# Attention of one item beside the feed-forward of the item two behind, in one order for all engines, with SiLU through tanh

## Time and profile before

| | us |
|---|---|
| median of 3 runs | 1201.09 |
| lowest, highest | 1197.25, 1201.25 |
| the profiled execution | 1206.52 |
| its span | 1204.7 |
| mean granted clock of TensorE | 0.762 |

### The profile page before, as it was taken

The page is one execution under the profiler, slowest core; times in us unless marked ns, Lnnn a source line. Parts: engine busy times, 40 slices in busy tenths (PEclk is TensorE's granted clock), DMA queues, the critical chain, the costliest instruction groups (busy, mean ns, idle before and its releaser), DMA issues. The chain is left out here.

```text
span 1204.7 us, 14263 instructions
## 1 busy us (share of the span) xinstructions
PE 1005.4 (83%) x5034; PEld 656.7 (55%) x5034; DVE 552.0 (46%) x1203; ACT 440.4 (37%) x649; POOL 261.5 (22%) x375
## 2 busy tenths in 40 slices
PE   3788777858658888779999788788789999999986
PEld 3534333225534444338888563433348888888874
DVE  2644453313344454424554544454434454534458
ACT  2344443332205434452343225444442332322240
POOL 7201032214314442211110104241110010101044
PEclk9666675567766555568999995655579999999997
DMA  5001010110001101110000002201210000000001
GB/s 126 2 1 19 1 19 2 18 18 16 1 0 54 37 1 36 36 18 9 1 1 1 1 13 64 43 14 35 40 21 5 1 1 1 1 1 1 1 1 35
DMA packets 24715, 21.01 MB, mean 17 GB/s; under 512 B 6559, under 2 KB 19847, under 8 KB 24519
## 3 DMA queue, kind: packets, MB, share of 16 engines
q1 hardware_dynamic: 24647, 20.10, 7.8%
...
HBM read 12.33 MB, written 1.05 MB: 11 GB/s over the span
## 5 line engine op out<-in xcount | busy, mean ns | idle before, releaser
L1134 DVE TENSOR_REDUCE mneg<-PS 128x4 f32<-128x624 f32 (+1 forms) x192 | 170.7, 894 | 180.5 <-PE PS L751 180.2
L1546 ACT ACTIVATE work<-PS 104x1024 f32<-104x1024 f32 (+1 forms) x160 | 163.5, 1022 | 182.4 <-PE PS L833 180.6
L1286 DVE TENSOR_TENSOR work<-PS,work 128x512 f32<-128x512 f32 (+2 forms) x168 | 114.8, 685 | 211.4 <-PE PS L885 134.9
L1576 ACT ACTIVATE work<-PS 128x512 f32<-128x512 f32 (+2 forms) x168 | 99.9, 597 | 243.5 <-PE PS L885 241.5
L902 PEld LDWEIGHTS PS<-down_w,work 128*128 128x128 f32 (+2 forms) x1472 | 175.4, 194 | 6.2 <-DVE work L1286 1.0
L902 PE MATMUL PS<-down_w,work 128*128 128x128 f32 (+2 forms) x1472 | 175.9, 277 | 0.7 <-DVE work L1286 0.7
L883 PE MATMUL PS<-xh_sb,arena 128*128 128x512 f32 (+2 forms) x352 | 152.6, 433 | 9.5 <-DVE work L1286 9.2
L848 PE MATMUL PS<-work,vb_sb 104*32 104x512 f32 (+1 forms) x640 | 147.6, 1014 | 3.4 <-ACT work L1546 3.4
L885 PE MATMUL PS<-xh_sb,arena 128*128 128x512 f32 (+2 forms) x352 | 142.8, 406 | 0.0
L884 PE MATMUL PS<-xl_sb,arena 128*128 128x512 f32 (+2 forms) x352 | 142.4, 405 | 0.0
L751 PE MATMUL PS<-kb_sb,qxt_sb 49*128 49x312 f32 x256 | 69.5, 530 | 57.9 <-DVE mneg L1134 52.7
...
## 6 DMA issues: line engine op xcount, KB each, us to landing
...
```

The source lines that it names most:

```text
L1134: dve.tensor_reduce(to, PS[:, bank:bank + 2, 0:HB * head_width(layer)].rearrange("p f (n h) -> p f h n", h=HB), AX.X, ALU.max, negate=True ...
L1286: dve.tensor_tensor(HH[0:rows, e % 2, j, :], PS[0:rows, 2 * (n % 2) + 1, :], SS[0:rows, n % 2, :], ALU.mult).then_inc(*sig["h"].mark((i, n)))
L1546: act.activation(P[0:rows, m % P_RING, :, :], PS[0:rows, 0:2, :], ACT.Exp, scale=SCALE).then_inc(*sig["p"].mark((i, m)))
L1576: act.activation(SS[0:rows, n % 2, :], PS[0:rows, bank, :], ACT.Silu).then_inc(*sig["act"].mark((i, n)))
```

## The change

`plan`, `all_slots` and the loops over `ITEMS` go. `step_pieces(s)` lists the pieces of one of 15 steps with a place for each, sorted by place, and each engine runs this one list. Step s holds attention item s (for s up to 11) and feed-forward item s - 2 (for s from 2 to 13), with the layer norm and preparation of attention item s + 1, parts of s + 2, and the end of attention s - 1 with the preparation of its feed-forward. The items of layer 3 are placed in steps 12, 13 and 14.

Banks: scores 0 and 1 as before; maxima, transposes, projections and router 2 and 3; values 4 alone (the score pairs are reordered so that one half of the heads is finished and evacuated before the other); first product of a tile 5 alone, second 6, both for GELU in turn; down projection 7 alone. `hidden` and the tanh output get space of their own, and `xn` and `xT` have one place for attentions and one for feed-forwards. The splits of the weights move to steps 4 to 10 (`w`), with the down weights of layer 2 in six groups (`wd`), each behind the last reader of the place that it takes; SP's queue issues them in the order of the list. SiLU is computed as 0.5 x (1 + tanh(0.5 x)): Tanh on ScalarE, then `silu` and the product on VectorE. The start of the kernel (the preparation of items 0 and 1) stays but for its banks. The space that the program keeps for DMA descriptors made at run time is set to 1024 bytes.

```diff
+N_ATT = 3 * B
+SKEW = 2
+N_STEPS = N_ATT + SKEW + 1
+BANK_MX, BANK_PV, BANK_UP, BANK_Y, BANK_F3 = 2, 4, 5, 7, 0
...
+def attention_pieces(a, put):
+    i = item_of(a)
+    N, C = n_slots(i), quads(i)
+    W = width(a)
+    scale = W / 29.0
+    for m in range(N // 2):
+        put(2 * m, "st", i, m)
+    for u in range(2 * C):
+        put(4 * u + 5, "pv", i, u)
+    put(4 * C + 2.5, "evac", i, 0)
+    put(N + 3, "evac", i, 1)
+    if a + 1 < N_ATT:
+        n, j = a + 1, item_of(a + 1)
+        if a == 0:
+            put(0.1, "kt", n)
+        for h in range(HB):
+            put(h + 0.2, "kb", n, h)
+        if n < B:
+            first, last = 5.1, N - 0.9
+            for g in range(G):
+                put(1.2 + g, "qxt", n, g)
+        else:
+            if n >= 2 * B:
+                for t in range(T):
+                    put(1.4, "ln", j, t)
+                put(1.5, "norm", j)
+            at = (4.2, 5.2, 5.3, 6.2, 6.3, 8.1, 8.3, 8.4) if n >= 2 * B else (1.4, 2.4, 2.5, 3.4, 3.5, 5.4, 5.8, 5.9)
+            for x, name in zip(at, ("xt", "q", "q1", "q2", "q3", "q4", "qsplit", "qlow")):
+                put(x, name, j if name == "xt" else n)
+            qx = 9.6 if n >= 2 * B else 8.4
+            for g in range(G):
+                put(qx + 0.7 * g, "qxt", n, g)
+            first, last = qx + 3.0, N + 2.4
+        for m in range(N_MAX):
+            put(first + m * (last - first) / N_MAX, "max", n, m)
+        put(first + (N_MAX - MT_LAST + 0.6) * (last - first) / N_MAX, "mt", n, 0)
+        put(N + 2.7, "mt", n, 1)
+        put(N + 1.5, "v", n)
+    if a + 2 < N_ATT:
+        n, j = a + 2, item_of(a + 2)
+        for x, name in ((10.3, "kproj"), (10.4, "k1"), (12.4, "k2"), (13.4, "k3"), (N - 2.2, "ksplit"), (N - 1.2, "klow"), (N + 4, "kt")):
+            put(x, name, n)
+        if n < B:
+            for t in range(T):
+                put(0.3 + t, "ln", j, t)
+            put(3.3, "norm", j)
+            for x, name in ((7.2, "xt"), (9.1, "q"), (9.2, "q1"), (11.1, "q2"), (12.1, "q3"), (16.1, "q4"), (17.1, "qsplit"), (18.1, "qlow")):
+                put(x, name, j if name == "xt" else n)
+        elif n < 2 * B:
+            for t in range(T):
+                put(20.5 * scale, "ln", j, t)
+            put(20.6 * scale, "norm", j)
+def ffn_pieces(f, W, put):
+    i = ffn_item(f)
+    kind = ITEMS[i][0]
+    tiles = ffn_tiles(kind)
+    if kind == "F0":
+        for n in range(4):
+            put(1.7 + 2.2 * n, "up", i, n, 0)
+        put(W * 0.45, "down", i, 0)
+        put(W * 0.45 + 1, "acc", i, 0)
+        return
+    for n in range(len(tiles)):
+        put(W * (n + 0.3) / len(tiles), "up", i, n, 0)
+        put(W * (n + 0.55) / len(tiles), "silu", i, n)
+        put(W * (n + 0.8) / len(tiles), "up", i, n, 1)
+    for e in range(tiles[-1][0] + 1):
+        last = max(n for n, tl in enumerate(tiles) if tl[0] == e)
+        x = W * (last + 2.1) / len(tiles)
+        put(x, "down", i, e)
+        put(x + 0.3, "acc", i, e)
+def ffn_prepared(f, W, put):
+    j = ffn_item(f)
+    s = W / 29.0
+    for t in range(T):
+        put(11.5 * s, "ln", j, t)
+    put(11.6 * s, "norm", j)
+    if ITEMS[j][0] == "F0":
+        put(14.2 * s, "rows", j)
+    put(15.2 * s, "xt", j)
+    put(15.3 * s, "after_xt", j)
+    for n, x in enumerate((18.3, 20.0, 22.0)):
+        put(x * s, "late", j, n)
+def step_pieces(s):
+    placed = []
+    def put(x, *piece):
+        placed.append((x, len(placed), piece))
+    W = width(s)
+    if s in (2, 6):
+        put(1.3, "bv", s // 4 + 1)
...
+    if s < N_ATT:
+        attention_pieces(s, put)
+    if SKEW <= s < N_ATT + SKEW:
+        ffn_pieces(s - SKEW, W, put)
+    if 1 <= s <= N_ATT:
+        j = item_of(s - 1)
         for t in range(T):
+            put(3.1 + t, "recip", j, t)
+        put(7.3, "normal", j)
+        put(9.3, "finish", j)
+        ffn_prepared(s - 1, W, put)
+    if s == 12:
+        attention3_pieces(0, 0.8, put)
+        ffn3_pieces(0, 23.6, 30.0, put)
+    if s == 13:
+        attention3_pieces(1, 0.8, put)
+        attention3_pieces(2, 9.0, put)
+        ffn3_pieces(1, 9.9, 17.0, put)
+        ffn3_pieces(2, 18.0, 25.0, put)
+    if s == 14:
+        attention3_pieces(3, 0.8, put)
+        ffn3_pieces(3, 9.0, 16.0, put)
+    return [piece for _, _, piece in sorted(placed, key=lambda p: p[:2])]
...
+            def up(i, kt, m):
                 kind, layer, b = ITEMS[i]
-                e, col, rows, slot = ffn_tiles(kind)[kt]
-                bank = 2 * (kt % 2)
-                if kt == 0:
+                tiles = ffn_tiles(kind)
+                e, col, rows, slot = tiles[kt]
+                j = kt - min(n for n, tl in enumerate(tiles) if tl[0] == e)
+                bank = BANK_UP + (kt % 2 if kind == "F0" else 0)
+                if kt == 0 and m == 0:
                     pe.wait_ge(*sig["xl"].at(i))
                     if kind == "F0":
                         pe.wait_ge(*sig["lora_l"].at(i))
-                    elif b == 0:
-                        pe.wait_ge(*sig["w_l"].at(len(weight_chunks(1)) - 1 if layer == 1 else 8 + len(weight_chunks(2)) - 1))
-                for m in range(1 if kind == "F0" else 2):
+                if kind != "F0" and b == 0 and j == 0:
+                    pe.wait_ge(*sig["w_l"].at(weight_serial(layer, e)))
+                if bank + m in taken:
                     pe.wait_ge(*taken[bank + m])
-                    taken[bank + m] = sig["h_gelu" if kind == "F0" else "h"].at((i, kt))
-                for m in range(1 if kind == "F0" else 2):
-                    if kind == "F0":
-                        w = [W1E[:, b % 2, hl, col:col + rows] for hl in range(2)]
-                    else:
-                        w = [UP(layer)[:, m, hl, col:col + rows] for hl in range(2)]
-                    o = PS[0:rows, bank + m, :]
-                    pe.matmul(o, w[0], xH[:, i % 2, :], start=True, stop=False)
-                    pe.matmul(o, w[0], xL[:, i % 2, :], start=False, stop=False)
-                    pe.matmul(o, w[1], xH[:, i % 2, :], start=False, stop=True).then_inc(*sig["up"].mark((i, kt, m)))
+                taken[bank + m] = sig["h_gelu" if kind == "F0" else "h" if m else "silu"].at((i, kt))
+                cols = slice(j * 128, j * 128 + rows) if layer < 2 or e < E2 else slice(j * 88, j * 88 + rows)
+                if kind == "F0":
+                    w = [W1E[:, b % 2, hl, col:col + rows] for hl in range(2)]
+                else:
+                    w = [up_weights(layer, m, hl, e)[:, cols] for hl in range(2)]
+                o = PS[0:rows, bank + m, :]
+                pe.matmul(o, w[0], xH[:, b % 2, :], start=True, stop=False)
+                pe.matmul(o, w[0], xL[:, b % 2, :], start=False, stop=False)
+                pe.matmul(o, w[1], xH[:, b % 2, :], start=False, stop=True).then_inc(*sig["up"].mark((i, kt, m)))
...
+            def silu(i, n):
+                rows = ffn_tiles(ITEMS[i][0])[n][2]
+                dve.wait_ge(*sig["act"].at((i, n)))
+                dve.scalar_tensor_tensor(SS[0:rows, n % 2, :], SS[0:rows, n % 2, :], 1.0, PS[0:rows, BANK_UP, :],
+                                         ALU.add, ALU.mult).then_inc(*sig["silu"].mark((i, n)))
+            def hidden_product(i, n):
...
+                dve.wait_ge(*sig["silu"].at((i, n)))
+                dve.wait_ge(*sig["up"].at((i, n, 1)))
...
+                dve.scalar_tensor_tensor(HH[0:rows, e % 2, j, :], SS[0:rows, n % 2, :], 0.5, PS[0:rows, BANK_UP + 1, :],
+                                         ALU.mult, ALU.mult).then_inc(*sig["h"].mark((i, n)))
...
-                    act.activation(SS[0:rows, n % 2, :], PS[0:rows, bank, :], ACT.Silu).then_inc(*sig["act"].mark((i, n)))
+                    act.activation(SS[0:rows, n % 2, :], PS[0:rows, BANK_UP, :], ACT.Tanh, scale=0.5).then_inc(*sig["act"].mark((i, n)))
...
+            for s in range(N_STEPS):
+                for p in step_pieces(s):
+                    piece(p)
```

944 lines of the change are left out of this document (433 added, 511 removed).

## The result

The changed kernel takes **1300.9 us** (median of 4 runs, 1299.6 to 1304.6) beside 1199.2 for the kernel before on the same chip: ratio 1.086, interval 1.082 to 1.089. It is 8.6% slower, where the forecast was 8% faster and the range ended at 1200. In the set of experiments 5 to 8 the nine executions of the kernel before took 1179 to 1208 us and the ratios use the three fastest of them, 1179 to 1189; with all nine they would be 1.025, 1.085, 1.043 and 1.039.

A forecast was written before the change was run, and what follows sets the result against it. Attention was held by TensorE's waits for row maxima and exponentials at a low clock, the feed-forward by TensorE itself. Start 54, steps 0 to 13 and 36 for step 14 summed to 1109 us of span, 1105 as median; range 1005 to 1200.

The forecast's parts named there:

- The start: Preparation before step 0: stays at 54 us.
- the chain of a tile: Feed-forward tile on one first-product bank: matmuls, tanh, VectorE step and back take 2.45 us, where a tile takes 1.38 today.
- GELU's share: Steps 2 to 5: table switches take 10 us of ScalarE a step, about 5 of which reach TensorE.
- rival D: Tanh is not in exp's table, so switches cost 206 us of ScalarE; 1205 to 1310 us, chance 0.03.
- Steps 10 and 11: Attention with layer 2's feed-forward: VectorE's work, about 3.0 us a tile, gives 98 us each, between 84 and 122.
- Steps 0 and 1: Attention alone: today's work, 49 us, plus 1 for maxima sharing banks 2 and 3 with projections; 50 us each.
- Steps 2 to 5: Attention with layer 0's feed-forward: TensorE's busy time, GELU switches and 5 for other waits; 68 and 62.5 us.
- Steps 6 to 9: Attention with layer 1's feed-forward: 3.3 us per tile plus down projections and clock; 73 us each, between 64 and 90.
- Steps 12 and 13: Layer 2's last feed-forwards: one-bank tile chain gives 85 us each, layer 3's items costing nothing in the gaps; 71 to 100.
- B: TensorE before first products and maxima: turns don't overlap, a step of 6 to 9 takes 90 us; total 1235, chance 0.13.
- C in its strong form: Merged steps: the clock falls to 1.2 GHz for half their time; total 1227 us, chance 0.04.
- Its milder form: Merged steps: a fifth to a third of the time at the low clock; total 1150 to 1195 us, chance 0.13.

The follow-up runs named there:

- experiments 5 to 8: In order: kernel before with tanh SiLU, 1.039; also single bank pair, 1.101; changed kernel with small products' banks apart, 1.058; also two pairs in steps 12, 13, 1.054.
- experiment 3: Changed kernel with GELU of layer 0 replaced by tanh, so without its table loads: 1282.7 us, ratio 1.076.
- Experiments 1 and 2: In order: kernel before with small products sharing the maxima's banks, 1282.0 us, 1.076; changed kernel with these banks apart in steps 0 and 1, 1273.5 us, 1.069.
- run 7: Changed kernel with most small products out of the maxima's banks in all steps up to 11: 1250.3 us, ratio 1.058.
- Experiment 10: Changed kernel without the added VectorE instruction, a factor of SiLU left out of the computation: 1239.0 us, ratio 1.037.
- experiment 8: Changed kernel with most small products' banks apart up to step 11 and two pairs of banks in steps 12 and 13: 1245.9 us, ratio 1.054.
- run 12: Changed kernel with banks apart to step 5, second first-product bank in 6 to 11, two pairs and later layer 3 in 12, 13, paired GELUs: 1251.5 us, 1.047.
- run 14: Changed kernel with banks apart to step 9, paired GELUs; in steps 12, 13 two pairs, later layer 3 and SiLU itself: 1218.8 us, ratio 1.017.
- experiments 1, 4 and 6: In order: kernel before with shared banks, 1.076; changed kernel with feed-forward products behind attention's, 1.250; kernel before with tanh SiLU and single bank pair, 1.101.
- experiment 4: Changed kernel with feed-forward products placed behind those of attention in every step up to 11, not interleaved: 1489.2 us, ratio 1.250.

## Why the prediction was wrong

**Right.** The start; the chain of a tile (2.45 us, measured 2.37); GELU's share (5 us a step, measured 19.4 over four, with the doubt of experiment 3); tanh in exp's table, which settles rival D; 33 loads; a clock of 0.85 or more from step 6 to 13; TensorE's busy time in steps 2 to 5 (58 and 54.5, measured 59.4 and 53.7 as means). The added VectorE instruction took 0.68 us, not 0.75.

**Right by luck.** Steps 10 and 11 were to take 98 each because VectorE's work for a tile sets the pace. They took 101.1 and 87.2, with VectorE busy for 69.7 and 54.0 us and TensorE for 90.4 and 81.1, where I had 81: TensorE's own work bounds them, and without the VectorE step they lose only 10 us of 188.

**Steps 0 and 1, +35.** The step that failed is "plus 1 for each because the maxima now share banks 2 and 3 with the projections". It named the cause and priced it at nothing. Experiments 1 and 2 priced it from both sides: 9 us an item, and 12 to 28 us in these two steps. I counted instructions, and none is added. What is added is a turn: with the small product in a bank of its own TensorE runs it while VectorE reads a maximum; in the same bank the two alternate. With the banks apart the two steps still took 107 to 123 us where the same two items took 102 before; step 1 holds 207 matmul instructions where its item had 196, and the clock does the rest. The share of each is open.

**Steps 2 to 5, +60.** I took "5 more for other waits", with 5 for the table loads 10 us in which TensorE stands still; it stood still for 20 to 26 us in each step, 95 in all, with 38 of them behind maxima and 21 behind exponentials. Undoing the shared banks gave 25 of the 60 back; GELU was in the forecast. What is left after it, 76 us of idle time in run 7, is again mostly the maxima (33) and the exponentials (14): the short feed-forward of layer 0 doesn't fill these waits, for which the sum had 5 us a step.

**Steps 6 to 9, +71, the largest.** Two steps failed. The term of the sum is "3.3 us until the next may start": the tile that I followed met two maxima and no small product. Measured were 5.4 us from one tile's first product to the next, where 3.3 and the down products make 4.2. And the sum took TensorE's own work, 62 us a step, to fit inside that chain. Measured were 77 us of busy time a step, more than the whole 73. The 62 came from "busy time times clock is the work of a stage as it would stand at 2.4 GHz", and the matmuls shrink by less than the clock. Groups by line, TensorE, first the kernel before at clock 0.55 (361 to 534 us):

```profile
L848 PE MATMUL PS<-work,vb_sb 104*32 104x512 f32 x192 | 44.7, 1023 | 1.1 <-ACT work L1546 1.1
L833 PE MATMUL PS<-qxt_sb,kb_sb 51*104 51x512 f32 x96 | 32.6, 669 | 7.2 <-ACT work L1546 7.0
L751 PE MATMUL PS<-kb_sb,qxt_sb 49*128 49x312 f32 x96 | 26.9, 547 | 17.6 <-DVE mneg L1134 17.5
L731 PE MATMUL PS<-ident_sb,qx_sb 128*115 128x128 f32 x48 | 13.9, 450 | 0.0
```

and run 7 at clock 0.98 (549.1 to 631.6 us), the same four kinds:

```profile
L1006 PE MATMUL PS<-work,vb_sb 104*32 104x512 f32 x48 | 7.0, 663 | 0.0
L895 PE MATMUL PS<-kb_sb,qxt_sb 49*128 49x312 f32 x32 | 6.3, 388 | 2.3 <-DVE mneg L1261 2.1
L988 PE MATMUL PS<-qxt_sb,kb_sb 51*104 51x512 f32 x26 | 6.3, 478 | 0.0
L875 PE MATMUL PS<-ident_sb,qx_sb 128*115 128x128 f32 x16 | 2.7, 291 | 2.0 <-DVE x_res L1454 1.9
```

1023 to 663 ns, 669 to 478, 547 to 388, 450 to 291: factors of 1.40 to 1.55, where 0.98/0.55 is 1.78. TensorE is busy for 69.6 us in that step of run 7, almost at full clock, where I had 62. In the changed kernel the clock of the four steps is 0.87, with the busy time at 77. Experiment 10 puts 33 us of the 71 on the VectorE step, 9 as waits and up to 24 through the clock; for the shared banks no run shows a part that stands clear of the clock's own changes.

**Steps 12 and 13, +26.** "The items of layer 3 lie in the gaps; they cost nothing there." They are TensorE's own work (step 13, with two of them, has 9 us more busy time than step 12 with one), and what stands behind the VectorE step's wait is their layer norm's (experiment 8). With a second pair of banks and the layer norms' wait moved out the two take 177 us (run 12), and 165 with SiLU itself in place of tanh (run 14). That this lies near the forecast 170 is no support for it, which was for tanh and one pair.

**The rivals.** B, slower because the turns don't overlap, had 0.13 and was the nearest: its 90 us for a step of 6 to 9 is the number that came (90.8 on average), but not its mechanism. In B TensorE stands still while turns are laid end to end; measured it was busy for 77 of the 91 us, and its waits for VectorE were 166 us in the whole kernel, not past the 250 named as B's sign. B's place was too narrow too: it counted turns of tiles and maxima from step 6 on and none in steps 0 to 5, where 95 us of the loss against the forecast lie. C in its strong form didn't come. Its milder form, a fifth to a third of the time at 1.2 GHz, did come in steps 6 to 9: a mean clock of 0.87 between the levels 0.5 and 1.0 is a quarter of the time. In steps 10 to 13 the clock was 0.93 to 1.00.

As for the whole, in parts of the kernel before's 1199 us by the ratios of experiments 1, 4 and 6: the shared banks cost 0.076 (91 us), tanh with the single pair 0.101 (121 us; 102 if all nine executions of the kernel before are used), interleaving gives 0.164 (197 us) back, and what the un-interleaved order of experiment 4 costs beyond the first two, 0.250 - 0.076 - 0.101 = 0.073 (88 us), wasn't taken apart. This supposes that the two costs add up, which no run tested. The rest may hold preparations that ran beside the feed-forward before and now stand with the attention, and single banks for the values and the down products. Ratios of two sets go into this, so each term is uncertain by some 10 to 20 us.
